# Wide attention: the two half maxima merged by a reduce over one operand that writes bf16, instead of a two-operand minimum and a rounding on ScalarE

## What is computed

```python
def _L0_attn_ref(x, w_q, w_k, w_v, w_proj, b_proj, ln_gamma, ln_beta):
    q = split_heads(x @ w_q)              # NUM_HEADS, HEAD_DIM = (16, 64)
    k = split_heads(x @ w_k)
    v = split_heads(x @ w_v)
    scale = HEAD_DIM ** (-0.5)
    attn = jnp.einsum('bnqd,bnkd->bnqk', q, k) * scale
    attn = jax.nn.softmax(attn, axis=-1)
    o = jnp.einsum('bnqk,bnkd->bnqd', attn, v)
    o = o.transpose(0, 2, 1, 3).reshape(x.shape[0], x.shape[1], NUM_HEADS * HEAD_DIM)
    y = o @ w_proj + b_proj + x
```

## Time and profile before

| | us |
|---|---|
| median of 3 runs | 3452.64 |
| lowest, highest | 3450.25, 3453.23 |
| the profiled execution, span from first to last instruction | 3455.0 |
| its mean granted TensorE clock | 0.917 of full speed |

### The profile page before, as it was taken

The page is one execution under the profiler, slowest core; times in us unless marked ns, Lnnn a source line. Parts: engine busy times, 40 slices in busy tenths (PEclk is TensorE's granted clock), DMA queues, the critical chain, the costliest instruction groups (busy, mean ns, idle before and its releaser), DMA issues. The chain is left out here.

```text
span 3455.0 us, 66767 instructions
## 1 busy us (share of the span) xinstructions
PE 2862.4 (83%) x21143; PEld 1283.2 (37%) x21144; DVE 2338.1 (68%) x3360; ACT 1849.0 (54%) x3005; POOL 1552.6 (45%) x1224
## 2 busy tenths in 40 slices
PE   3999999999999996799965599999978932484994
PEld 1333333333333334633323122222226622352772
DVE  5666666666666663788886799999944348534663
ACT  2555555555555551154463399999973443244442
POOL 0898999899989996200000011110115625460000
PEclk9999999999999997899986699999999965696995
DMA  2111111111111113500003222222221151113001
GB/s 86 31 42 47 43 52 46 42 48 42 56 42 48 42 48 119 197 1 1 0 2 126 66 49 56 54 53 53 53 85 47 46 182 42 29 39 100 11 13 55
DMA packets 263894, 189.55 MB, mean 55 GB/s; under 512 B 148174, under 2 KB 209990, under 8 KB 262576
## 3 DMA queue, kind: packets, MB, share of 16 engines
q1 hardware_dynamic: 255568, 174.05, 17.6%
q0 software_dynamic: 8224, 14.24, 1.3%
HBM read 105.21 MB, written 67.55 MB: 50 GB/s over the span
## 5 line engine op out<-in xcount | busy, mean ns | idle before, releaser
L331 POOL TENSOR_TENSOR attn_esum<-attn_esum,attn_prob 128x1024 f32<-128x1024 f32 x384 | 904.7, 2356 | 30.3 <-ACT attn_prob L482 6.7
L553 DVE TENSOR_REDUCE attn_half_max<-attn_peek 128x2 f32<-128x1024 f32 x512 | 627.0, 1225 | 398.7 <-PE attn_peek L382 394.9
L482 ACT ACTIVATE attn_prob<-attn_score 128x1024 f32<-128x1024 f32 x512 | 512.5, 1021 | 247.4 <-PE attn_score L365 247.4
L848 ACT ACTIVATE attn_prob<-attn_score 128x512 f32<-128x512 f32 x1024 | 556.3, 596 | 73.2 <-PE attn_score L798 59.0
L865 DVE TENSOR_REDUCE attn_half_max<-attn_peek 128x2 f32<-128x1024 f32 x512 | 583.5, 1214 | 11.5 <-PE attn_peek L784 11.4
L412 PE MATMUL attn_acc<-attn_prob,attn_v 128*64 128x512 f32 x2048 | 487.9, 597 | 0.1
L814 PE MATMUL attn_acc<-attn_prob,attn_v 128*32 128x256 f32 x4096 | 328.2, 392 | 12.1 <-ACT attn_out L840 10.6
L1745 POOL DMA_INDIRECT sorted_x<-attn_sent_rows,attn_send x64 | 62.5, 976 | 556.0 <-PE attn_score L798 521.1
L784 PE MATMUL attn_peek<-attn_ke,attn_qe 48*128 48x512 bf16 x1024 | 203.0, 393 | 46.1 <-DMA attn_ke<-k 31.6
L382 PE MATMUL attn_peek<-attn_hi 64*128 64x512 f16 x1024 | 200.2, 388 | 34.3 <-DVE attn_half_max L553 34.3
L331 POOL TENSOR_TENSOR attn_esum<-attn_prob 128x1024 f32<-128x1024 f32 x64 | 151.6, 2369 | 127.0 <-ACT attn_prob L482 127.0
(11 more groups left out here) (532 smaller groups left out, 4576.0 us busy)
## 6 DMA issues: line engine op xcount, KB each, us to landing
attn_xb<-attn_x_all SPq DMA_DIRECT2D x66, 256.0 KB
attn_invB<-inv SPq DMA_DIRECT2D x64, 256.0 KB
o<-attn_out SPq DMA_DIRECT2D x32, 512.0 KB
out_o<-o SPq DMA_DIRECT2D x8, 2048.0 KB
mix_f<-picked SPq DMA_DIRECT2D x16, 512.0 KB, 7.3
experts_x<-sorted_x SPq DMA_DIRECT2D x112, 65.0 KB
attn_qe<-q SPq DMA_DIRECT2D x192, 32.0 KB
attn_ke<-k SPq DMA_DIRECT2D x192, 32.0 KB
```

The lines of the kernel that those rows point to most:

```text
L331: nc.gpsimd.tensor_tensor(own, before, prob[:, u % NPROB, :, :], ALU.add).then_inc(added, 1)
L482: nc.scalar.activation(prob[:, u % NPROB, :, :], score[:, u % 2, :, :], ACT.Exp).then_inc(exped, 1)
L553: V.tensor_reduce(half_max[:, half, :, t], peek[:], AX.X, ALU.max, negate=True).then_inc(maxed, 1)
L848: nc.scalar.activation(prob[:, n % NPROB, :], score[:, n % RING, :], ACT.Exp).then_inc(exped, 1)
```

## The change

`half_max` is laid out anew, [P, heads, KT, 2] in place of [P, 2, heads, KT]: the two halves of a tile of keys lie side by side, and `maximum` writes there. `merge` is a minimum over the innermost axis of that one operand, and writes bf16 straight into `nmax`. `round_maxima`, the tile `both` and the semaphore `rounded` are gone; `turn` waits for `merged`. The merge no longer waits for the rounding of the iteration before. Everything else, the order of the engines' work too, is as it was.

```diff
--- before.py
+++ after.py
@@ -191,8 +191,7 @@
         prob = st.sb("prob", [P, NPROB, heads, CH])
         esum = st.sb("esum", [P, 2, NC, heads, CH])
         shift, sel = st.sb("shift", [P, 2, SEQ], BF16), st.sb("sel", [P, P], BF16)
-        half_max, ones = st.sb("half_max", [P, 2, heads, KT]), st.sb("ones", [P, 32])
-        both = st.sb("both", [P, NC, heads, TPC])
+        half_max, ones = st.sb("half_max", [P, heads, KT, 2]), st.sb("ones", [P, 32])
         nmax, nmaxT = st.sb("nmax", [P, NC, BLK], BF16), st.sb("nmaxT", [P, NC, BLK], BF16)
         out = st.sb("out", [P, 2, NC, CH])
         sums, flat, invB = st.sb("sums", [P, CH]), st.sb("flat", [P, NC * heads * CH // P]), st.sb("invB", [P, NC, CH])
@@ -203,9 +202,9 @@
         peek = st.ps("peek", [P, heads, CH])
         acc = st.ps("acc", [P, CH])
         small = st.ps("small", [P, CH])
-        names = ("w_loaded", "w_stored", "all_hi", "all_lo", "consts", "made", "hi_ready", "lo_ready", "v_ready", "peeked", "maxed", "merged", "rounded",
+        names = ("w_loaded", "w_stored", "all_hi", "all_lo", "consts", "made", "hi_ready", "lo_ready", "v_ready", "peeked", "maxed", "merged",
                  "max_ready", "scored", "exped", "added", "weighed", "read_out", "summed", "sums_read", "inverted", "normed")
-        (w_loaded, w_stored, all_hi, all_lo, consts, made, hi_ready, lo_ready, v_ready, peeked, maxed, merged, rounded,
+        (w_loaded, w_stored, all_hi, all_lo, consts, made, hi_ready, lo_ready, v_ready, peeked, maxed, merged,
          max_ready, scored, exped, added, weighed, read_out, summed, sums_read, inverted, normed) = (st.sem(n) for n in names)
         sums_out, flat_in, inv_out, inv_back, out_stored = (
             st.sem(n) for n in ("sums_out", "flat_in", "inv_out", "inv_back", "out_stored"))
@@ -503,11 +502,6 @@
                     act.wait_ge(sums_out, DMA * NC * heads * i)
                 nc.scalar.activation(sums[:], small[:], ACT.Copy).then_inc(sums_read, 1)
 
-            def round_maxima(i, c):
-                act.wait_ge(merged, NC * i + c + 1)
-                nc.scalar.activation(nmax[:, c, 0:heads * TPC].rearrange("p (h t) -> p h t", h=heads), both[:, c, :, :], ACT.Copy
-                                     ).then_inc(rounded, 1)
-
             def body(i, slot, first, final):
                 for s in range(STEPS):
                     u = 2 * s
@@ -519,10 +513,6 @@
                         take(i + 1, 1 - slot, 1)
                     elif s == SUM_STEP + 1 and not first:
                         read_sums(i - 1, True)
-                    if TURN_AT.get(u) == 1:
-                        round_maxima(i, 1)
-                    elif TURN_AT.get(u) == 0 and not final:
-                        round_maxima(i + 1, 0)
                     exp(i, u + 1, first)
                     if s in BEFORE and not final:
                         take(i + 1, 1 - slot, BEFORE[s])
@@ -537,7 +527,6 @@
                 take(0, 0, n)
             act.wait_ge(all_lo, 3 + BATCH)
             act.wait_ge(consts, 4)
-            round_maxima(0, 0)
             exp(0, 0, True)
             iterations(act, body)
             read(NI - 1, 1, 1, False)
@@ -550,17 +539,16 @@
             def maximum(i, m):
                 t, half = divmod(m, 2)
                 dve.wait_ge(peeked, U * i + m + 1)
-                V.tensor_reduce(half_max[:, half, :, t], peek[:], AX.X, ALU.max, negate=True).then_inc(maxed, 1)
-
-            def merge(i, c, any_before):
+                V.tensor_reduce(half_max[:, :, t, half], peek[:], AX.X, ALU.max, negate=True).then_inc(maxed, 1)
+
+            def merge(i, c):
                 dve.wait_ge(maxed, U * i + (c + 1) * PER_HALF)
                 tiles = slice(c * TPC, (c + 1) * TPC)
-                if any_before:
-                    dve.wait_ge(rounded, NC * (i - 1) + c + 1)
-                V.tensor_tensor(both[:, c, :, :], half_max[:, 0, :, tiles], half_max[:, 1, :, tiles], ALU.min).then_inc(merged, 1)
+                V.tensor_reduce(nmax[:, c, 0:heads * TPC].rearrange("p (h t) -> p h t", h=heads), half_max[:, :, tiles, :], AX.X, ALU.min
+                                ).then_inc(merged, 1)
 
             def turn(i, c, any_before):
-                dve.wait_ge(rounded, NC * i + c + 1)
+                dve.wait_ge(merged, NC * i + c + 1)
                 if any_before:
                     dve.wait_ge(shift_out, DMA * BLOCKS * (NC * (i - 1) + c + 1))
                 V.transpose(nmaxT[:, c, :], nmax[:, c, :]).then_inc(max_ready, 1)
@@ -584,9 +572,9 @@
 
                 def then(u):
                     if MAX_AT.get(u) == 1:
-                        merge(i, 1, not first)
+                        merge(i, 1)
                     elif MAX_AT.get(u) == 0 and not final:
-                        merge(i + 1, 0, True)
+                        merge(i + 1, 0)
                     if TURN_AT.get(u) == 1:
                         turn(i, 1, not first)
                     elif TURN_AT.get(u) == 0 and not final:
@@ -615,7 +603,7 @@
             for m in range(U - LEAD):
                 maximum(0, m)
                 if m == PER_HALF - 1:
-                    merge(0, 0, False)
+                    merge(0, 0)
                 elif m == PER_HALF:
                     turn(0, 0, False)
             iterations(dve, body)
```

## The result

| | before | changed |
|---|---|---|
| median, us | 3452.86 | 3428.78 |
| lowest to highest | 3450.25 to 3453.23 (4 runs) | 3425.43 to 3429.78 (4 runs) |
| profiled span | 3455.0 | 3427.3 |
| ratio | | 0.993 (0.9916 to 0.9944) |

The changed kernel is 24.1 us faster, against 24.9 forecast; it was timed again beside the last experiments: 3431.65 against 3456.94 us, 0.9927 (0.9913 to 0.9941). In the changed kernel's rows L381 is `look`, L542 `maximum`, L547 `merge`, L560 `take_low`, L554 `turn`, L481 `exp`, L419 the sum and L330 POOL's add. The tile t that `look` and `half_max` count is one of 128 queries; what lies side by side in the new `half_max` are the maxima over the two halves of the keys.

A forecast was written before the change was run, and what follows sets the result against it. TensorE, 98% busy at 38.73 us an iteration, was taken to set the wide attention's pace. Removing its stall, 29 x 0.86 = 24.9 us, takes the span from 3455.0 to 3430.1, less 2.4: 3427.8 us, range 3422 to 3435.

The forecast's parts named there:

- Point 1: VectorE's new merge, a reduce over one SBUF operand, takes 0.17 us, bounds 166 and 253 ns.
- Rival B: The one-operand merge still waits for POOL's add, keeping 1.2 and 2.2 us; time stays 3452.6 us; chance 0.03.
- Point 2: TensorE's stall behind one of two merges per wide-attention iteration goes: 29 x 0.86 = 24.9 us.
- Point 3: At the old stall, the maximum ends 0.29 us before the next look is due; margin next to none.
- Rival D: Maximum, writing 16 elements apart, lengthens; from 0.10 us on costs over 24.9 us; at 0.2 us, 3479; chance 0.02.
- Points 4 and 5: ScalarE's dropped roundings (upper bound 13.4 us) and the transpose now waiting for the merge: each worth 0.
- rival C: The maxima's transfers or the weighing's exp come 0.43 us late per iteration, 29 times: 3440.1 us; chance 0.03.
- point 4: ScalarE's 64 roundings of 0.21 us go, 13.4 us, but TensorE shows no wait for exp: worth 0.
- Point 6: POOL, next behind TensorE, keeps 1.4 of 2.31 us idle per iteration and would bind at 36.4 us.
- The sum: 24.9 us, all from the stall: span 3455.0 becomes 3430.1, less 2.4 to the median, 3427.8 us.

The follow-up runs named there:

- e2: Changed kernel with the merge again a minimum over two SBUF operands, writing bf16, still without ScalarE's rounding: 3456.58 us, ratio 1.0001.
- e4: Changed kernel with two operands only in the merge of the second half, c = 1, reduce for c = 0: 3454.54 us, ratio 0.9997.
- e8: Kernel before, with each of POOL's adds made as two of 128x512: 3440.78 us, ratio 0.9958.
- e3: Changed kernel with two operands only in the merge of the first half, c = 0, reduce for c = 1: 3431.17 us, ratio 0.9929.
- e6: Changed kernel with an extra VectorE reduce of 1792 constant elements behind the c = 1 merge: 3454.64 us, ratio 0.9997.
- e7: Changed kernel with a 16-element reduce (0.17 us) ahead of each even maximum: 3431.49 us, ratio 0.993.
- e11: Changed kernel with a 256-element reduce (0.42 us) ahead of each even maximum: 3465.99 us, ratio 1.0025.
- e1: Kernel before with the new layout and one-operand reduce merge, but in f32 with ScalarE's rounding and its wait kept: 3429.84 us, ratio 0.9925.
- e9: Changed kernel with one more POOL add of 128x1024 f32 per iteration, an unused tile to itself: 3438.57 us, ratio 0.9948.
- e10: Changed kernel with a small exponential ahead of ScalarE's wait for the first scores, loading the table early: 3432.20 us, ratio 0.9932.

## Why the prediction was right, point by point

Forecast 3427.8 (the terms give 3452.64 - 24.9 = 3427.7), measured 3428.78; both the mechanism and the size hold.

**Point 1**, the new merge at 0.17 us: 169 to 170 ns, all 64, beside a POOL that is busy 94% of the time. The line drawn through the reduces of 64 and 128 elements held at 16. Rival B fell: in the nine profiles with the one-operand merge everywhere it never took more than 173 ns. This is what the Trainium skill says ("SBUF — State Buffer", section "Who interferes with whom"), and what no row of before had shown; the trace of after agrees. That two operands wait again, and by the length of POOL's operation, is shown by e2, e4 and e8. Nor is a reduce of this size the dearer operation: 169 ns against the 166 of the unhindered merge.

**Point 2**, 29 x 0.86 = 24.9 us: the 29 iterations are 1123.20 - 1098.62 = 24.6 us shorter, 0.85 each. The forecast took the 0.86 of one stall for all 29; in the trace of before merges of 2.15 to 2.18 us alternate with ones of 2.05 for most of the stage, and a look behind one of 2.05 is 0.83 us late. Pricing the stall from start to start was needed; by the booked idle time it would have been 19.5. That the c = 0 merge costs nothing is e3, that the c = 1 merge costs all is e4. The onset was put at 1.2 us; merges and delays of all lengths place it at 1.2 to 1.3 (before, e6, e8).

**Point 3** was right in its result, wrong in its margin. The maximum ends 0.29 us before the next look, and the prediction called this margin next to none. e7 and e11 put the room at 0.25 us: the matmul, not its weight load, is what must not be late. Rival D's break-even of 0.10 us a maximum was thus wrong. Where it lies no run shows; it is below 0.34 us, for in e11 that much at the even maxima alone cost 34.3 us, by way of `take_low` too, which the prediction's sum for D left out and behind which there is hardly any room (0.09 us cost 0.08 in e7). Rival D itself fell: the maximum takes 1225 to 1228 ns in the changed kernel.

**Points 4 and 5**, the rounding and the transposition worth 0 each: right by e1, which keeps the rounding at the same iteration of 37.88 us. With it fell rival C: in the steady part of the changed kernel no matmul is seen to wait for `shift` or for `exp`. But point 4 counted the instructions and not what hung on the first of them, which stood in the prologue: without it the table load changed its place, +0.7 us from first look to first sum (0.6 of it in the gap ahead of the matmul of 88.02). The sum took the prologue as unchanged without a word on it; that is its one missing term.

**Point 6**, POOL's idle piece at 1.4 us, is 1.56 in the trace of after; the forecast took all of the 0.86 us from this piece, and a second one of about 0.2 us, which it hadn't counted, gave its share. POOL as the next bound is shown by e8 and e9; the forecast had it bind at a period of 36.4 us, e9 puts its own work at 36.1, and that it is paid in the tail, not in the iteration, is e9 as well.

**The sum.** 24.6 us won in the steady part, 0.7 lost ahead of it, 0.2 behind it (82.82 us from the last sum of that stretch to POOL's first instruction of the next stage, then 83.01): 23.7, and the medians are 24.1 apart. The profiled spans are 27.7 apart; of the other 4.0 us 0.2 lie ahead of the first look and 3.8 in later stages, which the change doesn't touch and which last 2103.9 to 2115.4 us over the fourteen profiles. That the median lies within 1 us of the forecast is therefore partly luck; that the steady part does is not.

## What to carry to other kernels

A small VectorE operation whose length varies by ten times is waiting inside its own bar: look at what POOL runs then, and whether it ends with POOL's operation. Here two SBUF operands are what made it wait; the same arithmetic over one operand (halves laid side by side, reduced over the innermost axis) doesn't, at the same 0.17 us. Ask where the wait falls before pricing it: here one of two merges of the same shape cost everything and the other nothing, and of 83 us of VectorE's time 25 came through. And when the last instruction ahead of a new activation function goes, look where its table load ends up.

## What the runs showed of the hardware that I had not expected

- A VectorE operation that waits for POOL's adds may pass the end of one and wait for the next when POOL starts the second 0.04 us before the first ends (e8: merges of 1.91 us beside adds of 1.27, up to 3.16). With POOL's pause of 0.08 us for a semaphore it got in.
- A POOL add of a tile to itself into itself took 1893 ns for 128x1024 f32, one of two tiles 2356 (e9).
- A weight load can come 0.16 us ahead of its matmul instead of the usual 0.22 without delaying it, and a maximum 0.25 us later than usual is the most that the next look forgives (e7, e11).
- The load of the exponential's table took 1.28 us and stood behind the last wait ahead of the first exponential: with the rounding ahead of that wait it was hidden, without it not.
- The distance of 512-column matmuls in the prologue went from 0.43 to 0.22 us at a point that isn't the same in every profile: 23.9 us after the first look in e10, 25.7 in the kernel before. Half a microsecond of a prologue can't be priced without looking for it.
